# Two MLPs with their down projections in plain fp32 instead of three reduced-precision products

## What is computed

```python
t = _to_tokens(x)
t = t + _L1_ffn_ref(_ln_t(t), ...)       # layer norm over the 256 channels first

# inside _L1_ffn_ref: 8 experts, the best 2 for each token, hidden width 256
logits = x @ w_router.T
expert_weight, expert_idx = jax.lax.top_k(softmax(logits), 2)     # weights divided by their sum
inter = jnp.square(jax.nn.relu(jnp.einsum('ecd,efd->ecf', binned, w1_stack)))
outb = jnp.einsum('ecf,edf->ecd', inter, w2_stack)                # experts' down projection
# and one shared expert for all tokens, hidden width 512
sh = jnp.square(jax.nn.relu(jnp.einsum('btc,fc->btf', hidden_tensor, ws1)))
shared_out = jnp.einsum('btf,cf->btc', sh, ws2)                   # shared down projection
return shared_out + moe_out
```

## Time and profile before

| | |
|---|---|
| median of 3 runs | 1235.08 us (1234.25 to 1237.88) |
| the profiled execution, its own time | 1227.22 us |
| its span | 1225.3 us |
| PE busy | 1055.8 us (86% of the span) |
| DVE, ACT, POOL busy | 628.6, 527.9, 263.3 us |
| second router, experts, shared expert | about 864 to 962, 962 to 1101, 1106 to 1223 us |

### The profile page before, as it was taken

One profiled execution on the slowest core, in us unless ns is written; L12 is line 12 of the kernel. 1 busy time (PEld: TensorE's weight loads), 2 busy tenths in 40 slices (PEclk: granted clock), 3 DMA queues, 4 the chain that ended last, 5 costly groups with the idle time before them and its releaser, 6 DMA issues. The chain is left out here.

```text
span 1225.3 us, 20877 instructions
## 1 busy us (share of the span) xinstructions
PE 1055.8 (86%) x5980; PEld 909.3 (74%) x5980; DVE 628.6 (51%) x1683; ACT 527.9 (43%) x1328; POOL 263.3 (21%) x274
## 2 busy tenths in 40 slices
PE   6965679999999999933899999987576799998998
PEld 6955668888888888832566666665476699987997
DVE  5388643222233222227556664343668355545887
ACT  6037354434344344423555443310455466663333
POOL 0000022111112111037422000000000444425664
PEclk9999999999999999976999999965555799998999
DMA  9533511111111111155211000000450244435553
GB/s 357 218 124 117 172 31 48 57 52 56 53 52 52 54 54 53 39 185 179 65 35 35 1 2 1 1 1 1 147 162 1 86 139 139 139 112 141 153 149 109
DMA packets 65222, 109.40 MB, mean 89 GB/s; under 512 B 10035, under 2 KB 47541, under 8 KB 64246
## 3 DMA queue, kind: packets, MB, share of 16 engines
q1 hardware_dynamic: 51894, 72.40, 16.8%
q0 software_dynamic: 12960, 35.41, 10.5%
q10 hardware_dynamic: 288, 0.47, 0.1%
HBM read 72.85 MB, written 35.39 MB: 88 GB/s over the span
## 5 line engine op out<-in xcount | busy, mean ns | idle before, releaser
L579 POOL DMA_INDIRECT experts_rows_sb<-h_rows,ids_i x142 | 134.0, 944 | 788.4 <-POOLq L522 460.5
L766 DVE TENSOR_TENSOR experts_a_sb<-experts_a_sb,experts_bankU 128x512 f32<-128x512 f32 x71 | 48.9, 689 | 224.1 <-PE experts_bankU L178 224.1
L719 ACT ACTIVATE experts_a_sb<-experts_bankG 128x512 f32<-128x512 f32 (+1 forms) x142 | 69.7, 491 | 91.6 <-PE experts_bankG L178 91.4
L710 ACT ACTIVATE experts_hT<-experts_bankH 128x256 fp32r<-128x256 f32 x142 | 54.2, 382 | 89.8 <-PE experts_bankH L639 89.7
L732 ACT ACTIVATE experts_y_sb<-experts_bankY 128x256 f32<-128x256 f32 x142 | 54.6, 384 | 88.1 <-PE experts_bankY L175 65.5
L908 POOL DMA_INDIRECT attn_y<-y_rows,pos_i x64 | 63.4, 991 | 100.7 <-DVE x_res L1243 48.1
L176 PE MATMUL attn_bankC<-attn_padded,attn_w_half 128*128 128x512 f32 x144 | 74.5, 517 | 8.6 <-ACT attn_feat L1146 4.4
L587 POOL DMA_INDIRECT shared_routed_sb<-y_rows,pos_i x64 | 65.6, 1025 | 62.2 <-DVE x_res L789 34.0
L175 PE MATMUL experts_bankY<-down_plain,experts_aT_plain 128*128 x284 | 72.9, 379 | 0.0
L330 PE MATMUL moe_bankT<-konst_sb,xn 128*128 128x128 f32 x128 | 34.8, 431 | 43.6 <-DVE xn L386 43.6
L181 DVE TENSOR_TENSOR experts_aT<-experts_bankA,experts_aT 128x256 fp32r<-128x256 f32 x142 | 59.6, 420 | 24.0 <-ACT experts_aT L727 24.0
(11 more groups left out here) (345 smaller groups left out, 3000.6 us busy)
## 6 DMA issues: line engine op xcount, KB each, us to landing
y_rows<-experts_y_sb SPq DMA_DIRECT2D x142, 128.0 KB, 1.8
h_rows<-xn SPq DMA_DIRECT2D x32, 256.0 KB, 2.4
x_res<-in_x SPq DMA_DIRECT2D x4, 1024.0 KB, 12.0
mix_xT<-in_xt SPq DMA_DIRECT2D x4, 1024.0 KB, 13.9
gate_raw<-in_L_ffn_gate_w SPq DMA_DIRECT2D x1, 4096.0 KB, 13.8
up_raw<-in_L_ffn_up_w SPq DMA_DIRECT2D x1, 4096.0 KB, 23.3
x_rows<-x_res SPq DMA_DIRECT2D x16, 256.0 KB, 2.5
x_res<-x_rows SPq DMA_DIRECT2D x8, 512.0 KB, 7.9
```

The costliest lines, as they stand in the source:

```text
L579: nc.gpsimd.indirect_dma_start(rows[t % DEPTH][:, :], None, h_dram, bass.IndirectOffsetOnAxis(ap=ids_i[:, t:t + 1], axis=0)).then_inc(s_ro ...
L719: nc.scalar.activation(a_sb[i % RING][:, :], bankG[i % RING][:, 0:hidden], ACT.Silu if gate is not None else ACT.Relu).then_inc(s["act"], 1)
L766: nc.vector.tensor_tensor(a_sb[i % RING][:, :], a_sb[i % RING][:, :], bankU[i % RING][:, 0:hidden], ALU.mult).then_inc(s["a"], 1)
```

## The change

`down1` and `ws2` become single fp32 tiles that SP loads whole, in two transfers (`load_down1`: 2 MB and 0.5 MB) between the first four stage loads and the first store of the second router. The router splits 10 pieces, one in each of n = 0 to 9. `mlp` gets one tile for `down` and so takes its other branch: one fp32 matmul for each chunk instead of three fp32r ones, one copy of `bankA` by DVE, none by ACT. PE waits for the two loads before each MLP. No other stage is touched.

```diff
@@ -1796,17 +1796,21 @@
-            up1, down1, ws1, ws2 = ([sb(f"{name}_{n}", [P, width], HALF) for n in range(2)]
-                                    for name, width in (("up1", E * KC * I1), ("down1", E * I1 // P * C), ("ws1", KC * IS), ("ws2", IS // P * C)))
+            up1, ws1 = ([sb(f"{name}_{n}", [P, width], HALF) for n in range(2)] for name, width in (("up1", E * KC * I1), ("ws1", KC * IS)))
+            down1, ws2 = ([sb(name, [P, width])] for name, width in (("down1", E * I1 // P * C), ("ws2", IS // P * C)))
+
+            def load_down1(sp):
+                sp.dma_start(down1[0][:, :], A["L1_ffn_w2_stack"]).then_inc(loads["down1"], 16)
+                sp.dma_start(ws2[0][:, :], A["L1_ffn_ws2"]).then_inc(loads["ws2"], 16)
             with ExitStack() as staging:
...
-                          for name, (high, low) in (("L1_ffn_w1_stack", up1), ("L1_ffn_w2_stack", down1), ("L1_ffn_ws1", ws1), ("L1_ffn_ws2", ws2))
+                          for name, (high, low) in (("L1_ffn_w1_stack", up1), ("L1_ffn_ws1", ws1))
                           for at in range(0, high.shape[1], step)]
-                router("moe1", router1, "router1", Halves("w1", pieces, stage))
-            mlp("experts1", SLOT_TILES, I1, up1, down1)
-            mlp("shared", TILES, IS, ws1, ws2, experts=False, sink=out)
+                router("moe1", router1, "router1", Halves("w1", pieces, stage), first=load_down1)
+            mlp("experts1", SLOT_TILES, I1, up1, down1, load=(("down1", 16),))
+            mlp("shared", TILES, IS, ws1, ws2, load=(("ws2", 16),), experts=False, sink=out)
```

More of the change, by code:

```diff
@@ L165, in build @@
         gate0_raw, up0_raw = (sb(f"{name}0_raw", [P, E * KC * I0], on=moe0_raw) for name in ("gate", "up"))
-        loads = {n: nc.alloc_semaphore(name=f"loaded_{n}") for n in ("konst", *(f"x{c}" for c in range(CHUNKS)), *(f"xt{c}" for c in range(CHUNKS)), "spectral", "router0", "gate0", "up0", "down0", "down0_plain", "router1", "conv", "attn")}
+        loads = {n: nc.alloc_semaphore(name=f"loaded_{n}") for n in ("konst", *(f"x{c}" for c in range(CHUNKS)), *(f"xt{c}" for c in range(CHUNKS)), "spectral", "router0", "gate0", "up0", "down0", "down0_plain", "router1", "conv", "attn", "down1", "ws2")}
         def x_tile(j, width=C, n=1):
```

## The result

The changed kernel takes **1248.42 us** (median of 5 runs, 1246.2 to 1251.58) beside 1237.25 us (1234.25 to 1240.66) for the kernel before in the same session. The ratio is 1.0092, with a 95% interval from 1.0065 to 1.0119, which is 11.4 us more (8.0 to 14.7). In a later session the same two kernels gave 1.0087 (1.0067 to 1.0106). The profiled execution of the changed kernel took 1246.2 us, its span is 1244.2.

What follows compares the result with a forecast made beforehand. It took PE's own work to bound both MLPs, and stalls on stores to lengthen the second router. 11.4 + 10.2 - 0.5 - 6.2 = +14.9 us on a median of 1235.1 gave 1250.0 us, range 1243 to 1258.

Steps and rivals of the forecast that it cites:

- The fp32 record: Down products of both MLPs: records start 0.217 us apart, so a chunk costs 0.434 instead of 0.354, 0.080 more.
- Down projection of the experts: Second experts: 71 tiles x 2 chunks x 0.080 us, all showing because PE is the bound, +11.4 us; tile 0.16 longer.
- Shared expert: Shared expert's down projection: 32 tiles x 4 chunks x 0.080 us, +10.2 us; a tile every 3.79 us.
- Drains: Last tiles of each MLP: the chain transpose, copy, down projection loses ACT's link, -0.5 us, between 0 and -1.5.
- The copies: bankA in both MLPs: ACT loses its copy, DVE's plain copy costs at most the old subtraction; neither matters.
- The router's stalls: Second router, pair 2 to 15: halved splits leave 4.3 of 10.7 us stalls; ACT's store waits fall well under 14.7.
- The router's bulk loads: Second router's start: 2.5 MB ahead of store 0 delays pair 2 by about 0.2 us, at most 3.
- Waits added: PE's wait for down1 before the experts and SP's two issues before store 0: nothing.
- The router gives nothing back: Second router: bulk loads delay first stores and DVE's work holds pairs, so steps only shift; 1256.2 us, chance 0.12.
- Four pitches: Down products of both MLPs: fp32 costs four fp32r pitches, 0.472 us a chunk, +31.9 us; 1260.3 us, chance 0.04.
- The clock rises: Second router: denser PE work lifts the clock from 1.2 to 2.4 GHz; 1242 us, chance 0.05.
- Weight loads set the pitch: Both MLPs: an fp32 record takes the 0.118 us weight-load pitch, -31.9 us; 1196.5 us, chance 0.04.

Runs made afterwards that it cites:

- mlp_alone: Kernel before with plain fp32 down projections in both MLPs, router still loading and splitting all 20 pieces, whole weights loaded after the walk: 1242.91 us, ratio 1.0122.
- after_again: The changed kernel measured and profiled once more, unedited, against the kernel before in a later session: 1240.5 us, ratio 1.0087.
- bulk_late: The changed kernel with the two bulk loads of down1 and ws2 issued after the second router's walk: 1236.79 us, ratio 1.0073 to the kernel before.
- stores_first: The kernel before with SP issuing a step's stage loads after the next pair's store: 1223.23 us, ratio 0.9957.

## Why the prediction was right, and where it was right by luck

Forecast 1250.0 us, measured 1248.42 in the session of the prediction; the sum was +14.9, measured +11.4 (8.0 to 14.7), so the predicted difference lies just outside the measured interval. The total came within 1.6 us because the kernel before took 1237.25 us over five runs and not the 1235.08 of three. The 7.9 us between a profiled execution and its timed runs did not carry over either: for the changed kernel they are 2.2, and the two profiled executions differ by 19.0. The likeliest case is the one that happened in kind: the products cost more than the router gives. By its own steps:

- **The fp32 record.** 0.217 us predicted from the first experts, 0.216 to 0.217 measured. The counts and the shared tile, 3.79 predicted and 3.77 measured, are right. This is the term on which the sign hung, and a row of the same form in the same kernel gave it. What it is compared with was read a little low: PE's own tile grew by 2.016 - 1.872 = 0.144 for two chunks, and the median tile of the shared expert from 3.473 to 3.766 for four, so a chunk costs 0.072 to 0.073 more and not 0.080. Two records take 0.432, and three products among their neighbours 0.36 where the prediction had 0.354.
- **Down projection of the experts, +11.4: the step that failed is "PE is the bound, so all of it shows".** It measured +6.6 to +7.2. I read a tile of 1.91 us and took 16 x 0.118 = 1.89 for a confirmation, though 1.91 was the mean of two tiles of 1.96 and 1.86 (the tile between the two in the earlier trace rows starts its down product at 1062.51). PE's work was 1.872, the rest gaps that longer products swallow: 3.0 us of the miss. Another 1.1 come from the 0.072 a chunk. The tile became 2.016, not 2.07. A tile of the experts "not longer by 0.16" was one of the prediction's own signs of being wrong, and it came: the tile is longer by 0.10.
- **Shared expert, +10.2.** Measured +9.6 in mlp_alone, +9.0 in after_again; 32 x (3.766 - 3.473) is 9.4. No gaps to swallow here.
- **Drains, -0.5.** The stretch between the MLPs takes 4.5 to 4.8 us in the six runs of the changed form and 4.8 to 5.8 in the seven with three products, 0.6 less in the mean. The size is right.
- **The copies.** Nothing, as taken, but DVE's copy is no cheaper than the subtraction: 415 ns. I left a fraction of it open. The Trainium skill, "VectorE: DVE Perf Modes", section "Why PSUM operands drop a tier", holds fp32 operands in PSUM at the base rate; the two equal durations agree.
- **The router's stalls, -6.4 of them.** Nearly right: -5.3 in the changed kernel, -5.9 in bulk_late, where the whole walk gains 6.5. The step from pair 3 to 4, 4.1 predicted, takes 4.62 and 4.18. But ACT's waits for stores did not "fall well under 14.7 us": they are 18.2, and 13.0 in bulk_late, while stores_first has them at 1.5 and gains less. Their sum does not tell what the walk loses.
- **The router's bulk loads, +0.2 and at most 3: mis-sized.** They cost 4.2 and 2.8 in the two profiles. The failed step is "with store 0 at 876.3": the prediction had them land 7 to 12 us after their issue and put the early end into its sum. They landed after 11.7 and 12.5 us (10.0 and 11.1 in after_again), and store 0 landed behind them, 9.6 us after its own issue (8.2). The issue at 869.45 instead of near 867 is no part of the miss, as the whole walk of this execution starts 3.0 us later. The net of the walk is therefore -1.1 (after_again -2.3) instead of -6.2.
- **Waits added, nothing.** Right: from pair 15 to the experts 40.35 against 40.38.

The products were 4 to 6 us too dear and the router's gain 4 to 5 us too large. The two errors cancelled; that the sum came out near is luck in good part, as is the kernel before that came out 2.2 us higher.

The rivals. *The router gives nothing back* named the right mechanism, bulk loads ahead of the stores, though the later steps did shorten; its 1256.2 is too high because the products were too dear and the router did give 1.1 to 2.3 us. *Four pitches* is out: an fp32 product costs two records of 0.216, 0.432, and not 0.472; the rule of the Trainium skill, "FP8 and Floating Point Precision", section "TensorE Precision Notes", gives the direction but not this size. *The clock rises* is out: from 868 to 926 the granted clock is 0.50, 1.2 GHz, with half the pieces as with all, also from 915 to 925, where PE is busy 10.00 of 10.00 us. The rule that sustained activity releases the clock (the Trainium skill, "TensorE: Matmul & The Clock Gate", section "What's actually happening") did not show itself in that row or in the earlier trace rows. Whether they contradict it is open: busy time counts latencies that overlap, 51 records in 10 us, and does not say how much of it the array worked. *Weight loads set the pitch* is out: 0.217, not 0.118.

**What stays open.** The stages of the profiled executions add up to +14.2 for the changed kernel (16.0 without the stages before the walk, less the one late step of 1.8) and +13.3 for after_again, the timed runs to +11.4 and +10.7. For bulk_late (+9.1 and +9.0) and mlp_alone (+15.5 and +15.0) the two agree. The bulk's cost may be smaller in most runs than in the profiled ones; no run here shows it. The expectation of after_again looked for the rest in a gain ahead of the router; its profile shows none, its pair 0 starts 2.4 us later than before. Why the first column moves, and what held the one late step of the shared expert, is open too.

## What to carry to other kernels

Before charging an edit on a "busy" engine in full, look at the spread of the tile's pitch and not at its mean: an uneven pitch holds gaps that longer work swallows. Issue a small transfer that someone waits for ahead of large ones and ahead of an issue that itself waits: here the order alone shortened the walk by 4.7 us, and halving the split work by 6.5. And the same instruction form elsewhere in the same kernel is the best price there is: read its pitch from starts, not from its duration.

## What the runs showed of the hardware that was not expected

- A 256 KB store behind 2.5 MB of loads landed after 9.6 and 8.2 us in the same queue, and after 7.0 us with the loads in another engine's queue and issued 1.8 us earlier; the 256 KB loads then took 8.5 us in the median instead of 4.2. 3.6 us is a store's median before.
- At a granted clock of 0.98 a fp32 product of 256 columns takes 0.432 us on PE, and three fp32r products 0.36 in the same place: 0.072 to 0.073 a chunk apart.
- Loading nine words of expert numbers into PE's registers delayed its first transpose by 3.1 us, recorded as "issue".
- DVE's plain fp32 copy from PSUM costs the same as a subtraction with PSUM and SBUF inputs: 415 ns for 128x256, 681 for 128x512.
- Removing register work from PE alone lengthened ACT's waits for the stores of y from 4.4 to 10.0 us: the experts became 1.3 us shorter, and 3.0 with four buffers besides.
